# Fused decoder layer: K and Q projected transposed, split into bf16 pieces and stacked by DMA through DRAM, context laid out transposed, scatter indices copied early

## The chip, the cores and the metric

The kernel runs on one core of one Trainium2 chip, as a single launch. The metric is the device time of that launch in microseconds (us). Engines are named as in the profile: PE (TensorE), PEld (its weight load), DVE (VectorE), ACT (ScalarE), POOL (GpSimd), SP (SyncE, which here issues nearly all plain DMAs).

## What is computed

Four sequences (B = 4) of T = 512 tokens with D = 256 features pass through three layers. Cut to what matters:

```python
x_norm = layernorm(x); beta = x_norm @ w_in.T              # 1: recurrence, gate, MLP
c = chunked complex recurrence over beta (chunks of 64)
x1 = x + sigmoid(x_norm @ w_gate.T + b_gate) * (c @ w_out.T)
x  = layernorm(x1 + silu(layernorm(x1) @ w_mlp1.T + b1) @ w_mlp2.T + b2)

Q = x @ wq.T + bq; K = ctx @ wk.T + bk; V = ctx @ wv.T + bv   # 2: attention, 16 heads of 16
scores = causal((Q @ K.T) / 4); attn = softmax(scores)
x = layernorm(x + (attn @ V) @ wo.T + bo)

logits = x @ Wr.T       # 3: 48 experts, each takes its top 64 of the 2048 tokens
out = x + scatter_add(weight * expert(x[chosen]))     # expert: 256 -> 4 x 256 -> gelu -> 256
return layernorm(out)
```

The scores must keep nearly float32 accuracy, so each K and Q value is split into three bf16 pieces (first piece, the rounded rest, the rest of that). A head has 16 features; six products of pieces, (0,0) (1,0) (2,0) (0,1) (1,1) (0,2), are taken in one matmul by stacking six copies of 16 rows into 96 contraction rows (`SK`). Three more rows (`SX` = 99) subtract the row maximum, itself in three pieces, in the second pass: ones on the K side, minus the maximum on the Q side.

## The kernel before

It is written with five instruction streams and semaphores placed by hand. Each stream runs in the order of the code.

**Stage 1** (recurrence and MLP) runs over the four sequences. Its last part, `shrink(B - 1)`, is the second MLP matmul of the last sequence; the buffers `KTs` and `QTs` (stacked K and Q, features on partitions) share memory with the MLP weights, so nothing may be written there before it ends.

**Stage 2** (attention) handles the 16 heads of a sequence in four groups of four (`NG`, `GH`), and a group in four slots, one for each block of 128 tokens. In slot (g, j) PE makes the shifted scores of block j of group g (`shifted`, L1618), ACT takes exponentials (`exponentials`, L1301), POOL masks the diagonal (L683), PE multiplies with V (`values`, L1631). In the same slots PE makes the plain scores of the *next* group (`scores`, L1584 and L1588, two PSUM banks in turn), DVE takes their row maxima (`maxima`, L986), then negates and splits them (`negate`), and PE turns them (`minus_max`, L1600, copied by ACT, L1288). The next group's scores come in three shares a slot; slot 1 has shares of 2, 1 and 1 banks, slot 2 has one share of 4 banks. After each share come the steps that two tables name: `PREPARE` (for the next sequence) and `FINISH` (for this one). A bank is written again only when its maximum has been taken.

The loop over sequences runs three times (`Fori(0, B - 1)`), each turn with the groups in order 1, 2, 3, 0; group 0 of the first sequence stands ahead of the loop and groups 1 to 3 of the last sequence behind it, and those three have no `PREPARE` or `FINISH` steps.

What `PREPARE` does before: `context` and `query_in` turn the inputs on PE (L1512, ACT copies L1251); `key`, `query` (L1530) and `value` (L1550) project them with tokens on partitions; DVE adds the bias (L918, L938) and with ACT splits into pieces (`split_k`, `split_q`: L926, L930, L932, L933, L947 to L956 on DVE, L1259 to L1271 on ACT); `stack_k` and `stack_q`, 8 steps each per sequence, turn the stacked pieces on PE (`pe_stack`, L1564, 8 transposes a step), and ACT (K, L1276) or DVE (Q, L973) copies them to `KTs` and `QTs`. For the first sequence these steps are lists: `early` ahead of `shrink(B - 1)`, `late` (12 stack steps) behind it.

**Stage 3** (experts) handles 48 experts in 24 pairs. A ring of six weight buffers is refilled by SP (2.5 MB a pair) as PE frees them. For a pair p, POOL gathers 64 + 64 token rows by indirect DMA (`gather`, L720 copy of the indices, L723 DMA), PE turns them (L1740) and runs the expert, DVE weighs the result (L1153), and POOL adds the rows to `sums` in DRAM (`scatter`, L730 copy of the indices, L735 DMA). POOL's order is scatter p, gather p + 6, wait until scatter p has landed (`after_addition`), and on to p + 1: two scatters may hit the same row.

**Stage 4** reads `sums` back, adds, normalizes and stores.

## Time and profile before

| | us |
|---|---|
| three runs | 839.89, 836.05, 840.32 (median 839.89) |
| the profiled execution | 844.63 |
| its span, first to last instruction | 842.9 |
| mean granted PE clock | 0.895 of full speed |
| stage 1 | 0 to about 203 |
| stage 2 | about 203 to 571 |
| choice of tokens | about 571 to 611 |
| experts | about 611 to 818 |
| final sum and norm | about 818 to 843 |

Times inside the profile count from the start of the span. Busy shares of the span: PE 77%, DVE 47%, ACT 37%, POOL 22%. Many engines wait for each other in turn, so no single share says what a step is worth.

### The profile page before, as it was taken

How to read it: one execution, taken by the hardware profiler on the slowest of the kernel's cores; microseconds unless marked ns; L12 is line 12 of the kernel's file. 1: busy time of each engine (PE TensorE's matmuls, PEld its weight loads, DVE VectorE, ACT ScalarE, POOL GpSimd, SP SyncE). 2: the span in 40 equal slices, each digit the busy share in tenths (PEclk: the TensorE clock that was granted, in tenths of full speed). 3: DMA queues.
4: the chain of work that ended last, by engine and by line, in shares of the span. 5: the costliest groups of instructions: out<-in, count | busy, mean ns of one | idle time of the engine just before them, and what ended most of it. 6: DMA issues, size and time to landing. Idle time of an engine off the chain costs nothing.

```text
span 842.9 us, 13300 instructions
## 1 busy us (share of the span) xinstructions
PE 645.3 (77%) x4550; PEld 397.2 (47%) x4550; DVE 399.3 (47%) x837; ACT 307.9 (37%) x490; POOL 188.7 (22%) x250
## 2 busy tenths in 40 slices
PE   4599999999688887877787887851079987898920
PEld 2458575767355554645554554340035444454410
DVE  4534442524757564675647655427823322233315
ACT  2141414142364563546355545610023322232303
POOL 1322231400212111121102111200032224234424
PEclk9899999999699799989998999965579988999965
DMA  6830000110000002000020007018249998994238
GB/s 221 325 133 2 0 0 0 51 51 1 0 2 1 1 2 88 12 0 0 18 81 0 0 0 274 2 35 313 110 153 374 407 313 284 359 343 125 40 62 260
DMA packets 33010, 93.64 MB, mean 111 GB/s; under 512 B 2720, under 2 KB 24912, under 8 KB 29904
## 3 DMA queue, kind: packets, MB, share of 16 engines
q1 hardware_dynamic: 27664, 86.43, 27.6%
q0 software_dynamic: 4608, 6.29, 4.0%
q10 hardware_dynamic: 704, 0.47, 0.3%
q8 instruction: 20, 0.33, 0.2%
q14 instruction: 14, 0.11, 0.0%
HBM read 79.55 MB, written 11.53 MB: 108 GB/s over the span
## 4 chain that ended last, share of the span: by engine, by line
PE 47%; DVE 17%; DMA 15%; issue 10%; ACT 6%; POOL 3%; DVEq 0%; ACTq 0%; POOLq 0%; SPq 0%
DMA sums<-row 7%; PE PS L1457 7%; PE PS L1448 7%; PE PS L1530 5%; DMA sums<-wo_s,row 4%; PE PS L1754 4%; DVE Mx L986 3%; PE PS L1631 3%; PE PS L1564 2%; PE PS L1588 2%; PE PS L1618 2%; DMA wkv_s<-x_rows,row 2%; PE PS L1419 2%; PE PS L1436 2%; ACT arena L1301 2%
## 5 line engine op out<-in xcount | busy, mean ns | idle before, releaser
L986 DVE TENSOR_REDUCE Mx<-PS 128x1 f32<-128x384 f32 (+3 forms) x176 | 107.4, 638 | 85.6 <-PE PS L1588 84.7
L1301 ACT ACTIVATE arena<-PS 128x512 f32<-128x512 f32 (+1 forms) x176 | 86.3, 565 | 73.9 <-PE PS L1618 73.9
L683 POOL TENSOR_SCALAR_AFFINE_SELECT arena<-arena 128x512 f32<-128x512 f32 x64 | 40.9, 640 | 241.6 <-ACT arena L1301 241.6
L1618 PE MATMUL PS<-arena 99*128 99x512 bf16 (+3 forms) x256 | 58.6, 317 | 23.8 <-ACT arena L1301 16.9
L1588 PE MATMUL PS<-arena 96*128 96x128 bf16 (+3 forms) x256 | 66.5, 318 | 0.0
L1143 DVE TENSOR_TENSOR X<-PS,Y 128x512 f32<-128x512 f32 x48 | 31.3, 687 | 71.8 <-PE PS L1767 71.5
L1584 PE MATMUL PS<-causal,identb 128*128 128x128 bf16 (+2 forms) x176 | 45.5, 259 | 20.4 <-DVE Mx L986 17.8
L1448 PE MATMUL PS<-arena 128*128 128x512 f32 x128 | 55.8, 593 | 1.6 <-issue 1.6
L1457 PE MATMUL PS<-arena 128*128 128x256 f32 x256 | 55.9, 379 | 0.0
L1365 ACT ACTIVATE X<-X 128x512 f32<-128x512 f32 x48 | 29.5, 631 | 71.4 <-DVE X L1143 71.0
L1457 PEld LDWEIGHTS PS<-arena 128*128 128x128 f32 x256 | 48.6, 190 | 6.6
L1631 PE MATMUL PS<-arena 128*32 128x128 f32 (+3 forms) x512 | 49.7, 458 | 1.4 <-POOL arena L683 1.2
L1136 DVE COPY X<-PS 128x512 f32<-128x512 f32 x24 | 16.6, 692 | 65.9 <-PE PS L1754 63.6
L1754 PE MATMUL PS<-ring_a,X 128*64 128x512 f32 x192 | 46.5, 628 | 0.5 <-ACT X L1354 0.5
L1618 PEld LDWEIGHTS PS<-arena 99*128 99x128 bf16 x256 | 21.8, 100 | 50.8 <-ACT arena L1301 29.4
L1754 PE MATMUL PS<-arena,X 128*64 128x512 f32 x192 | 44.7, 608 | 0.0
L1584 PEld LDWEIGHTS PS<-causal,identb 128*128 128x128 bf16 x176 | 17.6, 100 | 56.1 <-DVE Mx L986 42.3
L1276 ACT ACTIVATE arena<-PS 99x1024 bf16<-99x1024 bf16 x32 | 31.8, 1025 | 33.3 <-PE PS L1564 33.2
L617 POOL TENSOR_SCALAR ve<-mv 128x4 f32<-128x4 f32 x16 | 3.7, 230 | 179.8 <-DVE mv L790 179.8
L1448 PEld LDWEIGHTS PS<-arena 128*128 128x128 f32 x128 | 24.2, 190 | 30.2 <-issue 29.5
L1288 ACT ACTIVATE arena<-PS 3x1024 bf16<-3x1024 bf16 x32 | 31.1, 1010 | 19.7 <-PE PS L1600 19.6
L1203 ACT ACTIVATE arena<-PS,vec 128x512 f32<-128x512 f32 x16 | 11.4, 775 | 71.7 <-PE PS L1403 71.7
(195 smaller groups left out, 1151.5 us busy)
## 6 DMA issues: line engine op xcount, KB each, us to landing
ring_a<-experts SPq DMA_DIRECT2D x12, 2048.0 KB, 10.9
arena<-experts SPq DMA_DIRECT2D x12, 2048.0 KB, 11.3
ring_a<-experts SPq DMA_DIRECT2D x12, 512.0 KB, 5.3
arena<-experts SPq DMA_DIRECT2D x12, 512.0 KB, 8.2
X<-x SPq DMA_DIRECT2D x4, 512.0 KB, 3.7
arena<-w_mlp SPq DMA_DIRECT2D x2, 1024.0 KB, 11.6
sums<-zrow SPq DMA_DIRECT2D x1, 2048.0 KB, 20.3
Y<-ctx_in SPq DMA_DIRECT2D x4, 512.0 KB, 4.7
```

Of the source, the lines that this page charges most:

```text
L683: pool.affine_select(out=pb[j % 2][:, :, 0:P], in_=pb[j % 2][:, :, 0:P], compare_op=ALU.is_ge, fill=0.0, base=0, pattern=[[0, GH], [1, P]] ...
L986: dve.tensor_reduce(Mx[:, g % 2, i, heads[0]:heads[-1] + 1], bank((g * NSH + u) % 2)[:, 0:len(heads) * w] .rearrange("p (h n) -> p h n", h ...
L1276: act.activation(KTs[0:SX, GH * q:GH * q + GH, 2 * P * m:2 * P * (m + 1)], spare(n).bitcast(BF16)[0:SX, :] .rearrange("p (h n) -> p h n", ...
L1301: act.activation(pb[j % 2][:, heads[0]:heads[-1] + 1, 0:w], bank(2 + n % 3)[:, 0:len(heads) * w] .rearrange("p (h n) -> p h n", h=len(heads)),
L1448: mm = pe.matmul(bank(HIDDEN[m % 4]), wm1_s[:, k, m * P:(m + 1) * P], xT2[:, k, :], start=(k == 0), stop=(k == KT - 1))
L1457: mm = pe.matmul(PS[:, 6 * 512 + t * D:6 * 512 + (t + 1) * D], hid[:, m, t * P:(t + 1) * P], wm2_s[:, m, :], start=(m == 0), stop=(m == MT ...
L1530: mm = pe.matmul(o[:, t * D:(t + 1) * D], xt[:, k, (2 * m + t) * P:(2 * m + t + 1) * P], w[:, k, :], start=(k == 0), stop=(k == KT - 1))
L1584: pe.matmul(o[:, 0:len(heads) * w].rearrange("p (h n) -> p h n", h=len(heads)) [:, :, i * P:w], identb[:], wide(causal[:], len(heads)), st ...
L1588: mm = pe.matmul(o[:, a * w:(a + 1) * w], QTs[0:SK, g * GH + h, i * P:(i + 1) * P], KTs[0:SK, g * GH + h, 0:w], start=False, stop=True, sk ...
L1618: mm = pe.matmul(bank(2 + n % 3)[:, a * w:(a + 1) * w], KTs[0:SX, g * GH + h, j * P:(j + 1) * P], QTs[0:SX, g * GH + h, j * P:T], start=Tr ...
L1631: mm = pe.matmul(bank(6)[VW * h:VW * (h + 1), j * P:T], Vb[:, j, g * GH + h, :], pb[j % 2][:, h, 0:T - j * P], start=(j == 0), stop=(j == ...
L1754: mm = pe.matmul(bank(1 + n)[CAP * e:CAP * (e + 1), :], xgT[:, k, CAP * e:CAP * (e + 1)], w1_of[u][:, e, k, n * 512:(n + 1) * 512], start= ...
```

## The change

It does five things.

1. The context arrives transposed (its layout is made on the host side of the inputs), so `context` steps, their PE transposes and ACT copies are gone. SP loads it straight to `cT`.
2. K and Q are projected with features on partitions (`pe_features`, two matmuls of 512 columns instead of four of 256). ACT makes the first piece from PSUM with the bias (`first_piece`), DVE the rest (`rest`, one operation with bias and subtraction), ACT the middle piece, DVE the last piece.
3. The stacking steps are gone from PE, ACT and DVE. SP writes the three pieces of K and of Q to DRAM (`split_out`) and reads them back, a group at a time, into the six row blocks of `KTs` and of `QTs` (`group_in`, 12 DMAs of 64 KB, 16 partitions each). `scores` waits for these. POOL writes the rows of ones into `KTs` once.
4. `value 0` moves from slot (1, 3) to slot (2, 1), `query_in 1` one slot ahead; for the first sequence key is ahead of the second half of the last MLP expansion and all that is left is ahead of `shrink(B - 1)`.
5. In stage 3 the scatter indices of pair p + 1 are copied ahead of the wait for scatter p (`rows_of`).

```diff
 PREPARE = {
-    (1, 0): ([("context", 0)], [], [("context", 1), ("query_in", 0)]),
-    (1, 1): ([("query_in", 1), ("key", 0)], [("key", 1), ("split_k", 0)],
-            [("split_k", 1), ("query", 0)]),
-    (1, 2): ([("split_k", 2)], [("query", 1)], [("split_k", 3), ("split_q", 0)]),
-    (1, 3): ([], [("split_q", 1)], [("split_q", 2), ("value", 0)]),
-    (2, 0): ([("split_q", 3)], [], []),
-    (2, 1): ([("stack_k", 0), ("stack_k", 1)], [], [("stack_q", 0)]),
...
+    (1, 0): ([("query_in", 0)], [], [("query_in", 1)]),
+    (1, 1): ([("key", 0)], [("key", 1)], [("query", 0)]),
+    (1, 2): ([("split_k", 0)], [("query", 1)], []),
+    (1, 3): ([("split_q", 0)], [], []),
+    (2, 1): ([], [("value", 0)], []),
 }
 ENTER = {
     (0, 0): ([], [], [("value", 1)]),
-    (0, 2): ([("stack_k", 6)], [("stack_k", 7), ("stack_q", 6)], []),
-    (0, 3): ([], [("stack_q", 7)], []),
 }
...
+            def split_out(b):
+                for g in kq_in:
+                    sp.wait_ge(g.s, g.before(b, NRD))
+                sp.wait_ge(ksd.s, ksd.now(b, KT + 1))
+                sp.dma_start(pieces_v[0], kp).then_inc(k_out.s, 16)
+                sp.wait_ge(qsd.s, qsd.now(b, KT + 1))
+                sp.dma_start(pieces_v[1], qp).then_inc(q_out.s, 16)
+
+            def group_in(b, g):
+                if g == 0:
+                    sp.wait_ge(k_out.s, k_out.now(b, 1))
+                    sp.wait_ge(q_out.s, q_out.now(b, 1))
+                sp.wait_ge(stm.s, stm.before(b, (g + 1) * NSH))
+                heads = slice(GH * g, GH * g + GH)
+                rows_g = slice(GH * HD * (g % 2), GH * HD * (g % 2) + GH * HD)
+                for n, (dst, order) in enumerate(((KTs, K_PIECES), (QTs, Q_PIECES))):
+                    for r, c in enumerate(order):
+                        sp.dma_start(dst[HD * r:HD * r + HD, heads, :],
+                                     pieces[n, c, g // 2, rows_g, :]
+                                     .rearrange("(h d) t -> d h t", d=HD)).then_inc(kq_in[g].s, 16)
...
+            tokens_in(0)
+            context_in(0)
+            split_out(0)
+            tokens_in(1)
+            sp.wait_ge(m2.s, m2.now(B - 1, 1))
+            for g in range(NG):
+                group_in(0, g)
+            context_in(1)
+
+            def relay(b, more=True):
+                split_out(b + 1)
+                group_in(b + 1, 0)
+                if more:
+                    tokens_in(b + 2)
+                for g in range(1, NG):
+                    group_in(b + 1, g)
+                if more:
+                    context_in(b + 2)
+                    outputs(b)
...
+            pool.wait_ge(m2.s, m2.now(B - 1, 1))
+            for g in range(NG):
+                pool.memset(KTs[SK:SX, GH * g:GH * g + GH, :], 1.0).then_inc(ones, 1)
+            pool.wait_ge(ones, NG)
             with_bias(0)
...
+            rows_of(0, 0)
             with pool.Fori(0, NP // RING - 1) as r:
                 for u in range(RING):
                     p = r * RING + u
                     scatter(p, u)
                     gather(p + RING, u, again=True)
+                    rows_of(p + 1, u + 1)
                     after_addition(p)
...
+            def rest(read, done, parts, left, bias):
+                def step(b, m):
+                    dve.wait_ge(read.s, read.now(b, m + 1))
+                    dve.wait_ge(done.s, done.before(b, KT + 1))
+                    dve.scalar_tensor_tensor(left[:, m, :], spare(m), vec[:, bias + m:bias + m + 1],
+                                             parts[:, 0, m, :], ALU.add, ALU.subtract)\
+                        .then_inc(done.s, 1)
+            def last_piece(read, done, parts, left):
+                def step(b, k):
+                    dve.wait_ge(read.s, read.now(b, KT + 1))
+                    dve.tensor_tensor(parts[:, 2], left, parts[:, 1], ALU.subtract)\
+                        .then_inc(done.s, 1)
...
+            def middle_piece(done, read, parts, left):
+                def step(b, k):
+                    act.wait_ge(done.s, done.now(b, KT))
+                    act.activation(parts[:, 1], left, ACT.Copy).then_inc(read.s, 1)
...
+            def pe_features(o, w, xt):
+                for k in range(KT):
+                    mm = pe.matmul(o, w[:, k, :], xt[:, k, :], start=(k == 0), stop=(k == KT - 1))
...
-                        pe.wait_ge(ske.s, ske.now(b, 2 * (g + 1)))
-                        pe.wait_ge(sqe.s, sqe.now(b, 2 * (g + 1)))
+                        pe.wait_ge(kq_in[g].s, kq_in[g].now(b, NRD))
...
             minus_max(0, 0)
+            pe.wait_ge(ones, NG)
             slots(0, pe_slot, first=True)
```

How the instruction order moves, at three places. First DVE in the loop, slots (1, 1) and (1, 2), where `arena` and `ring_a` hold the K and Q values. Before, from K's first subtraction on to Q's second bias addition:

```order
L926 TENSOR_TENSOR arena<-arena 128x1024 [waits ksa]
L937 ISA [waits qpr]
L938 TENSOR_TENSOR ring_a<-PS,row 128x512 [waits qsd]
L985 REGISTER_ALU
L986 TENSOR_REDUCE Mx<-PS 128x1 [waits smm]
...
L938 TENSOR_TENSOR ring_a<-PS,row 128x512 [waits qsd,qpr]
```

The same place in the changed kernel:

```order
L955 SCALAR_TENSOR_TENSOR ring_a<-PS,vec,ring_a 128x512 [waits qsd,qsa]
L964 REGISTER_ALU
L966 TENSOR_TENSOR arena<-arena 128x1024 [waits ksd,ksa]
L990 REGISTER_ALU
L991 TENSOR_REDUCE Mx<-PS 128x1 [waits smm]
...
L955 SCALAR_TENSOR_TENSOR ring_a<-PS,vec,ring_a 128x512 [waits qsd,qsa]
```

K's last piece (L966), which waits for ACT's middle piece (`ksa`), now stands ahead of the four maxima of slot (1, 2). Before, nothing stood between Q's first bias addition and these four.

Second POOL behind stage 1, before:

```order
L617 TENSOR_SCALAR ve<-mv 128x4 [waits vset,ln3]
L619 TENSOR_TENSOR rstd<-ve,mhalf 128x4 [waits rs3]
L676 TENSOR_TENSOR X<-X,row 128x1024 [waits rs3,xs_in]
L683 AFFINE_SELECT arena<-arena 128x4x128 [waits exq] x4
L695 UNCONDITIONAL_BRANCH
```

and in the changed kernel:

```order
L648 TENSOR_SCALAR ve<-mv 128x4 [waits ln3]
L650 TENSOR_TENSOR rstd<-ve,mhalf 128x4 [waits rs3]
L723 MEMSET arena 3x2048 [waits rs3,m2]
L723 MEMSET arena 3x2048 x3
L704 TENSOR_TENSOR X<-X,row 128x1024 [waits ones,xs_in]
```

The four memsets of the rows of ones stand behind the last normalization's square root, and PE waits for them (`ones`) ahead of its first slot.

Third POOL in the experts' loop, before (`row` is the memory of the index copies and of the results):

```order
L720 COPY row<-Y 128x1
L721 REGISTER_ALU
L723 DMA wkv_s<-x_rows,row 128x256 [waits gix]
L741 REGISTER_ALU
L730 ISA [waits scattered]
L730 COPY row<-Y 128x1
L733 REGISTER_ALU [waits six]
L735 DMA sums<-row 4096x256 [waits yws]
```

and in the changed kernel:

```order
L755 DMA wkv_s<-x_rows,row 128x256 [waits gix]
L761 ISA
L761 COPY row<-Y 128x1
L775 REGISTER_ALU
L767 REGISTER_ALU [waits scattered,six]
L769 DMA sums<-row 4096x256 [waits yws]
```

The copy (L730, now L761) has moved from behind the wait for `scattered` to ahead of it.

## Rows read from the trace of the kernel before

**Rows 1.** The page, mean busy share of the DMA engines, 40 slices of 21.1 us, tenths.

```profile
DMA  6830000110000002000020007018249998994238
```

**Rows 2.** Busy time by stretch: span, then PE, PEld, DVE, ACT, POOL, clock, DMA share.

```profile
359.50:379.90 20.40, 15.52 (x137) 8.92 (x136) 13.98 (x29) 10.93 (x18) 3.03 (x5) 0.83 0.00 0
379.90:397.40 17.50, 13.79 (x152) 8.74 (x153) 10.32 (x21) 11.46 (x19) 2.55 (x4) 1.00 0.00 0
397.40:424.80 27.40, 21.63 (x179) 14.21 (x179) 14.63 (x37) 12.13 (x20) 3.85 (x6) 1.00 0.17 46
424.80:448.60 23.80, 21.42 (x161) 14.87 (x161) 15.92 (x25) 13.34 (x22) 5.05 (x5) 1.00 0.09 35
527.20:540.10 12.90, 10.61 (x96) 5.30 (x96) 7.86 (x17) 7.86 (x15) 2.55 (x4) 1.00 0.01 2
```

**Rows 3.** Groups of instructions by line, 356.3 to 445.6 us, one loop turn.

```profile
L1564 PE MATMUL PS<-identb,arena 128*99 128x128 bf16 x64 | 5.5, 243 | 0.6 <-DVE Y L1015 0.6
L1550 PE MATMUL PS<-wkv_s,arena 128*128 128x128 f32 x32 | 4.0, 278 | 0.0
L1512 PE MATMUL PS<-ident,Y 128*128 128x128 f32 x24 | 3.6, 277 | 0.8 <-DVE Y L1015 0.8
```

**Rows 4.** Timeline of the loop: start, us, engine, line, [idle before and releaser].

```profile
419.84 0.44 PE L1600 MATMUL PS<-identb,nst 128*3 128x128 bf16 x5 [1.59 <-DVE arena L973]
...
439.47 2.52 DVE L986 TENSOR_REDUCE Mx<-PS 128x1 f32<-128x512 f32 x4
439.95 1.06 ACT L1262 ACTIVATE arena<-arena 128x1024 bf16<-128x1024 f32 x1
444.37 1.23 DVE L930 TENSOR_TENSOR arena<-arena 128x1024 bf16<-128x1024 f32 x1
...
452.52 0.39 PE L1618 MATMUL PS<-arena 99*128 99x512 bf16 x1 [2.87 <-ACT arena L1301]
```

**Rows 5.** Timeline between stage 1 and the loop, PE and POOL.

```profile
166.50 1.81 POOL L659 MEMSET arena<- 128x2048 f32 x1
189.58 13.98 PE L1457 MATMUL PS<-arena 128*128 128x256 f32 x64
...
213.95 0.38 PE L1584 MATMUL PS<-causal,identb 128*128 128x512 bf16 x1 [0.83 <-DVE arena L973]
224.98 1.04 POOL L619 TENSOR_TENSOR rstd<-ve,mhalf 128x4 f32<-128x4 f32 x1
225.70 1.03 PE L1618 MATMUL PS<-arena 99*128 99x512 bf16 x2 [1.16 <-ACT arena L1288]
```

**Rows 6.** DMA to landing (the page), and SP's time for an issue (min/median/max ns).

```profile
x_rows<-ring_a SPq DMA_DIRECT2D x4, 512.0 KB, 3.0
L529 SPq DMA_DIRECT2D x_rows<-ring_a x4: 380/390/407, 330.1 to 565.9; - x4
```

**Rows 7.** Experts: timeline of scatters (POOL) and results (DVE), and PE's waits.

```profile
632.89 1.65 POOL L735 DMA_INDIRECT sums<-wo_s,row  x1 [9.63 <-DVE wo_s L1153]
...
645.13 1.61 POOL L735 DMA_INDIRECT sums<-wo_s,row  x1 [1.01 <-POOL row L730]
651.59 0.47 DVE L1153 TENSOR_SCALAR row<-PS,Y 128x256 f32<-128x256 f32 x1
658.27 0.47 DVE L1153 TENSOR_SCALAR row<-PS,Y 128x256 f32<-128x256 f32 x1
...
757.43 1.60 POOL L735 DMA_INDIRECT sums<-wo_s,row  x1 [1.01 <-PE PS L1740]
...
807.54 0.48 DVE L1153 TENSOR_SCALAR row<-PS,Y 128x256 f32<-128x256 f32 x1 [2.41 <-PE PS L1786]
PE PS L1740 <- DMA wkv_s<-x_rows,row: 22.4, 6, 5.8
```

**Rows 8.** The chain that ended last, in the tail of the scatters: start, us, what.

```profile
793.00 3.84 DMA sums<-wo_s,row
...
814.12 3.80 DMA sums<-row
```

More of the change, by code:

```diff
@@ L31 @@
 SX = SK + NPC
+K_PIECES = (0, 1, 2, 0, 1, 0)
+Q_PIECES = (0, 0, 0, 1, 1, 2)
+NRD = 2 * NPR
 VW = 32
@@ L468, in all_steps @@
             return [step for lists in table.values() for names in lists for step in names]
-        after = ("stack_k", 0), ("stack_q", 0)
-        first_steps = all_steps(PREPARE)
-        split_at = min(first_steps.index(step) for step in after)
-        early = [(name, 0, k) for name, k in first_steps[:split_at]]
-        late = [(name, 0, k) for name, k in first_steps[split_at:]]
+        early = [(name, 0, k) for name in ("query_in", "key") for k in range(KT)]
+        late = [("split_k", 0, 0), ("query", 0, 0), ("query", 0, 1), ("split_q", 0, 0),
+                ("value", 0, 0)]
         block = stack.enter_context(nc.Block())
@@ L533, in _ @@
             sp.wait_ge(res.s, res.now(B - 1, 3))
-            inputs(0)
-            with sp.Fori(0, B - 1) as b:
-                inputs(b + 1)
-                outputs(b)
-            sp.wait_ge(skt.s, skt.now(B - 1, 2 * NG))
+            tokens_in(0)
[16 more added lines that the diff above has]
+                    outputs(b)
+            with sp.Fori(0, B - 2) as b:
+                relay(b)
+            relay(B - 2, more=False)
+            weights(0, 0, second=False)
             sp.wait_ge(vpr.s, vpr.now(B - 1, 2))
+            outputs(B - 2)
             weights(3, 3)
-            sp.wait_ge(sqt.s, sqt.now(B - 1, 2 * NG))
-            weights(0, 0, second=False)
             outputs(B - 1)
@@ L958, in dve_value @@
+            def last_piece(read, done, parts, left):
+                def step(b, k):
+                    dve.wait_ge(read.s, read.now(b, KT + 1))
+                    dve.wait_ge(done.s, done.now(b, KT))
+                    dve.tensor_tensor(parts[:, 2], left, parts[:, 1], ALU.subtract)\
+                        .then_inc(done.s, 1)
+                return step
             def dve_value(b, m):
```

238 lines of the change are left out of this document (77 added, 161 removed).

## The prediction

> **What bounds the kernel now.** I read the slices of the page first, then busy time by stretch, then the timeline of the places that the change touches, then the waits. The DMA slices [rows 1] show where transfers can matter: nearly none in the attention (the tenth to the twenty-seventh slice), and 8 or 9 tenths through most of the experts' stage. In the attention no engine is full: a turn of the loop is a ring of PE, DVE, ACT and POOL, and its length is what the ring adds up to. The stretches of one turn [rows 2] are the measure: group 2 takes 20.4 us, group 3 17.5, group 0 27.4, group 1 23.8. The last sequence, whose groups have the same scores, maxima and exponentials but no step of either table, gives the bare group: 12.9 us. What a turn can win by losing steps is read against this number and not against busy shares.
>
> In the experts' stage PE waits for no weights. It waits for gathered rows: 22.4 us in 6 waits, of which 5.8 is the first fill [rows 7]. A gather is issued right behind a scatter, and a scatter only when the one before has landed and its index copy is done. So the scatters are a chain: the first starts at 632.89, the fourteenth at 757.43, 9.6 us apart, while PE undisturbed gives a result each 6.7 us (651.59, 658.27). In each link stand the copy, some 0.2 us, and the 1.01 us from its end to the DMA behind it, 1.2 in all [rows 7].
>
> **The attention loop, group by group.** *Group 2* loses five stack steps and gains `value 0`. Bare group plus one value step, half of the 4.0 us of L1550 [rows 3]: 14.9. The bare group runs at full clock; today's group 2 has a granted clock of 0.83 [rows 2], because DVE's split copies hold up the maxima and PE stands for 2.87 us [rows 4]. Both go. 20.4 to 14.9. *Group 3* loses seven stack steps and has nothing left: 17.5 to 12.9. *Group 0* keeps value, heads, output, norm, turn and logits and loses four stack steps: K's eight steps cost PE 5.5 us busy (L1564 [rows 3]), so four steps at most 2.8, less where they overlap; the 1.59 us wait for a stack copy [rows 4] also goes, but DVE's statistics hold the maxima there, so not all of both is won. I take 2.4: 25.0.
>
> *Group 1* is where the change can lose. It sheds the context's eight transposes (of 24 of L1512 in 3.6 us [rows 3], 1.2 busy, I take 0.9) and `value 0` (2.0, moved). But in slot (1, 2) K's last piece now stands ahead of four maxima on DVE and waits for ACT's middle piece, which waits behind two exponentials. I follow it with today's times, shifted by the 0.9: PE ends the slot's shifted scores at 438.1; ACT first owes Q's first piece, then exponentials to 439.4, then the middle piece (1.06, as L1262 today) to 440.5; DVE's last piece (1.23, as L930) to 441.8; so the first of the four maxima starts at 441.8 where today the four start at 439.47 [rows 4]. PE has two banks, so it stands from 438.7 to the end of the first maximum, 442.5: a hole of 3.8 us with nothing behind it in its queue that could run, for the second query projection stands behind the four scores. After that, query 1, its first piece on ACT, its rest on DVE, the negation, the turn of the maxima and ACT's copies follow in series, with ACT's middle piece of Q (1.06) ahead of the copies. My hand count puts the next group's start at 450.2 against 448.4 to 448.6 today, so group 1 is 25.4 at full clock. Today's hole of 2.87 us is followed by a lower clock; a hole of 3.8 probably is too, and I add 2.0 for matmuls at the low level (bounds 0 and 3.3, the time PE loses behind today's hole). Group 1: 27.4, from 23.8.
>
> Sum of a turn: 27.4 + 14.9 + 12.9 + 25.0 = 80.2 against 89.1, 8.9 saved; three turns: **27 us**. Without hole and low clock it would be 13 a turn (39). If only the 4.6 of group 3 and the 2.4 of group 0 came and the rest were eaten up by group 1, 5 a turn (15).
>
> **What the DMAs cost.** No row shows a 64 KB DMA onto 16 partitions. From below: SP issues in 0.39 us and 512 KB in 1 KB rows land in 3.0 [rows 6], so a group's twelve are 4.7 us of issue plus some 2.5 to land, 7 us. From above: each of the twelve takes its landing alone, 3.0, so 36 us. The last row blocks overlap in the queue as the weights do today, so I take the nearer end, 8 us. In the loop, Q's last piece is ready at about 449.5, the pieces' write lands some 5 us later, group 0's rows at 462.5, and PE wants them one bare group and a value step after 450.2, at 465. Margin 2.5 us: hidden, but only just. The other three groups are read a group or more ahead. SP's other DMAs wait behind these, but the context and token loads are wanted a group later.
>
> SBUF — State Buffer, a page of the Trainium skill, section "Door 1: The DMA port swizzle (why `[64,N]` ≈ `[32,N]`)", says that a transfer to partitions 0 to 15 reaches 4 of 16 ports, about 109 GB/s, and a later section of it that transfers to different partitions do not add up. By that rule a 64 KB transfer would hold the queue for 0.6 us (an estimate from the page's figure), twelve would take 7.2 plus the landing, and the rows would come about 1.5 us later than in my sum, still inside the margin; nothing in this trace shows it.
>
> **Between stage 1 and the loop.** Today `shrink` ends at 203.56, twelve stack steps follow, and the scores start at 213.95 [rows 5]. Then: the context's transposes and a wait are gone ahead of `shrink`, so it ends 1.7 us earlier, at 201.9; then one group's DMAs, 8 to 9.2 us: scores at 210.5, 3.4 earlier. PE stands longer and starts at the lower clock, which gives 0.7 back. But the first slot now waits for the ones. POOL writes them only after the root of the last norm, which ends at 226.0 today and 2.7 earlier then, at 223.3. The nearest memset is 128 x 2048 f32 in 1.81 us [rows 5]; 3 x 2048 bf16 has as many elements on a partition, so I take 1.75 each, four times: 7.0 (bounds: half of it, if bf16 goes twice as fast, and 7.2). PE starts at 230.5 where today it starts at 225.70, 4.8 later. Four stack steps less in that group and a norm that no longer holds DVE give 2.8 back. **Net +2** (from -3.6 to +5).
>
> **Experts.** The removed 1.2 us (I use 1.13, as a short check of the semaphore stays) stands in each link. Thirteen links up to the scatter at 757.43 make 14.7 us if the DMAs land as fast as today. They will not quite: a faster chain means that PE asks sooner for weights, and the DMA engines are 8 to 9 tenths busy [rows 1]. Bounds 0 and 14.7; I take 0.7 a link, **9 us**. In the tail the last result is ready at 808.02 while the last scatter starts at 814.12 [rows 7]: the last five scatters start 5.3 us apart (793.00 to 814.12 [rows 8]), so the chain lags behind PE's results. With links of 3.84 + 0.3 [rows 8] it catches up, the last two results 2.9 apart: the last scatter starts some 2 us behind its result and lands 3.9 earlier relative to PE. Experts together: **13 us** (4 to 19).
>
> **Sum.** -27 + 2 - 13 = -38. The profiled execution took 844.63 (span 842.9 and 1.7 around it), so 806.6. The median of the three runs is 839.89, 4.7 lower; the forecast for the median is **802**.
>
> **Rivals.**
> *The relay comes late (slower).* If a 64 KB DMA holds the queue for d us, group 0's rows come in 12 d + 2.5. Beyond d = 0.6 each turn loses 12 (d - 0.6) minus what is left of the margin (1.5), and the start loses the same once without margin. With d = 1.5 that is 3 x 9.3 + 10.8 = 39, and the saving of 38 is gone; with d = 1.7 it is 48, so 850. The page's port rule stands for d = 0.6 alone. For it speaks that a row block's descriptors all end on few partitions, against it that 512 KB in equally small rows land in 3.0 [rows 6], which is d = 0.4 even with the fixed part in it. 8%, 850.
> *Attention gives less.* The bare group is measured where SP is quiet and no table has steps; if group 1 stretches by a further 4 us, or the relay is a little late in each turn, the loop brings 12 and the total is 817. 14%.
> *The experts' chain gains nothing.* Every 1.13 us saved is given back by longer landings, since the DMA engines are the real limit; only the tail's 4 stay: 811. For it speak the 9 tenths [rows 1], against it that the first link took 12.2 us and the mean one 9.6 [rows 7]: later landings were much shorter, so the engines are not full throughout. 12%.
> *My forecast,* 66%, 785 to 812.
>
> **Range.** The least is all of the loop (39), 19 in the experts and 3.6 at the start: 62, 778. The most inside the eight in ten takes the rival of a weaker attention with half the experts' gain: 824. So 779 to 824. Faster or slower by 0.5% (4.2 us) is what a measurement can tell from no change. Faster: 0.66 + 0.14 + 0.12 less a little for their bad ends, 0.88; slower 0.08; same 0.04.
>
> **What the profile will show.** Group stretches of about 27, 15, 13 and 25 us, twelve DMAs of 64 KB at some 0.4 us issue each, no PE wait on them in the loop, a hole of 3 to 4 us on PE in slot (1, 2) with four maxima released by the last piece (L966), four memsets of about 1.75 us with PE waiting for POOL ahead of its first slot, scatter links 0.5 to 1 us shorter, and a last scatter within 3 us of the last result. I am wrong if PE waits for SP's DMAs at the first scores of a group, if group 2 and 3 stay above 16 and 14, or if the landings of the scatters grow by as much as the copy gave.

## The result and the profile after

The changed kernel takes 815.63 us (median of 4 runs, 810.62 to 816.48), the kernel before 840.07 (4 runs, 836.05 to 840.32): ratio 0.970 with a 95% interval of 0.966 to 0.974, so 24 us faster. The forecast was 802 with a range of 779 to 824. The profiled execution took 816.48, its span is 814.7 and its mean granted clock 0.884; it stands against the 844.63 of before, 28.2 less, where the sum had 38. All medians here are of executions in the chip's usual state; three slower ones (819.0 us of `e3_ones_early`, 931.7 and 843.7 us of the kernel before) are left out.

The page of the changed kernel, granted PE clock and busy share of the DMA engines by slices of 20.4 us, beside [rows 1]. The relay fills the tenth to the twenty-third slice with up to 4 tenths. The busiest slices of the experts' stage show 59999994 where they showed 49998994. (The 7 tenths of the twenty-fifth slice in [rows 1], which the prediction counts as nearly none, are the experts' first weights.)

```profile
PEclk9899999999569899989998989965589999898965
DMA  6840000003410341134113334018159999994247
```

Busy time by stretch in the changed kernel, the second turn of the loop in the order of groups 1, 2, 3, 0, then the bare group of the last sequence; columns as in [rows 2].

```profile
329.33:356.94 27.61, 21.02 (x120) 9.84 (x120) 13.19 (x23) 13.96 (x24) 2.55 (x4) 0.88 0.09 28
356.94:371.65 14.71, 12.36 (x111) 7.16 (x111) 8.74 (x21) 7.80 (x15) 4.89 (x5) 1.00 0.56 178
371.65:384.67 13.02, 10.58 (x96) 5.30 (x96) 7.86 (x17) 7.81 (x15) 2.55 (x4) 1.00 0.36 106
384.67:411.16 26.49, 21.03 (x147) 13.27 (x148) 13.50 (x35) 9.99 (x18) 3.80 (x6) 0.94 0.23 77
506.82:519.68 12.86, 10.60 (x95) 5.28 (x95) 7.86 (x17) 7.82 (x15) 2.55 (x4) 1.00 0.01 2
```

Read against [rows 2], groups 2 and 3 fell to the forecast's 14.9 and 12.9 within 0.2 us. Group 1 grew by 3.8 to 27.6 and its clock fell to 0.88. Group 0 won only 0.9, and its clock, 1.00 before, is 0.94: PE is busy for 21.03 us against 21.63, although four stack steps are gone (one took some 0.5). A turn is 81.8 us, before 89.1.

The timeline of the changed kernel, first between stage 1 and the loop, then slot (1, 2) of the second turn, then slot (0, 2) of the first. Each row is start, duration, engine, line, and in brackets the idle time before it with its releaser.

```profile
202.16 22.79 SPq L537 DMA_DIRECT2D arena<-pieces  x48
209.76 0.59 PE L1563 MATMUL PS<-causal,identb 128*128 128x512 bf16 x1 [7.63 <-DMA arena<-pieces]
223.02 6.09 DVE L837 TENSOR_SCALAR X<-X,mv,rstd 128x256 f32<-128x256 f32 x4 [1.58 <-POOL rstd L650]
223.30 7.55 POOL L723 MEMSET arena<- 3x2048 bf16 x4 [0.32 <-POOL rstd L650]
230.90 1.04 PE L1597 MATMUL PS<-arena 99*128 99x512 bf16 x2 [9.41 <-POOL arena L723]
...
344.98 1.23 DVE L966 TENSOR_TENSOR arena<-arena 128x1024 bf16<-128x1024 f32 x1 [1.17 <-ACT arena L1268]
346.12 1.28 DVE L991 TENSOR_REDUCE Mx<-PS 128x1 f32<-128x512 f32 x2
346.86 0.29 PE L1563 MATMUL PS<-causal,identb 128*128 128x128 bf16 x1 [3.57 <-DVE Mx L991]
347.97 3.62 PE L1526 MATMUL PS<-arena,wq_s 128*128 128x512 f32 x4
...
317.13 1.41 DVE L824 BATCH_NORM_STATS2 stats<-ring_a 128x6 f32<-128x256 f32 x4
318.99 2.49 DVE L991 TENSOR_REDUCE Mx<-PS 128x1 f32<-128x512 f32 x4
319.70 0.23 PE L1563 MATMUL PS<-causal,identb 128*128 128x128 bf16 x1 [2.59 <-DVE Mx L991]
```

These are the places that the forecast named. The scores begin at 209.76 (forecast 210.5), the first slot at 230.90 behind the memsets (forecast 230.5). In slot (1, 2) K's last piece (L966) runs ahead of the maxima and PE stands 3.57 us (forecast 3.8); behind it the four matmuls of the second query projection (L1526) take 3.62 us, elsewhere 1.88: the low level, 1.2 GHz. The last block is what the forecast saw only in part: DVE's statistics and aggregation stand ahead of the maxima of slot (0, 2) too, as they did before, and the hole that PE has there has grown to 2.59 us.

The experts in the changed kernel, scatters (POOL) and the last result (DVE), beside [rows 7, 8].

```profile
611.00 1.65 POOL L769 DMA_INDIRECT sums<-wo_s,row  x1 [9.30 <-DVE wo_s L1157]
...
729.71 1.60 POOL L769 DMA_INDIRECT sums<-wo_s,row  x1 [4.03 <-issue]
...
782.30 0.48 DVE L1157 TENSOR_SCALAR row<-PS,Y 128x256 f32<-128x256 f32 x1 [3.47 <-PE PS L1762]
784.39 1.57 POOL L769 DMA_INDIRECT sums<-row  x1 [2.99 <-DMA sums<-row]
```

From the first to the fourteenth scatter it is 118.7 us, before 124.5: 9.13 a link against 9.58, so 0.45 won where the forecast took 0.7. The last scatter starts 2.1 us behind the start of its result's row, before 6.6.

### The profile page after: what moved, and what is told of

The parts are those of the page before. It is cut to its first block, busy times and chain, and to the rows that moved or that the text cites. A ratio compares the mean times of both kernels' runs of the same rounds, so it can differ in the third digit from the quotient of the medians.

```text
span 814.7 us, 12126 instructions
## 1 busy us (share of the span) xinstructions
PE 612.5 (75%) x3942; PEld 351.0 (43%) x3942; DVE 358.4 (44%) x777; ACT 274.5 (34%) x458; POOL 195.1 (24%) x253
## 4 chain that ended last, share of the span: by engine, by line
PE 49%; DMA 16%; DVE 15%; issue 9%; ACT 7%; POOL 3%; SPq 1%; ACTq 0%; DVEq 0%; POOLq 0%
DMA sums<-row 9%; PE PS L1451 7%; PE PS L1442 7%; DMA sums<-wo_s,row 4%; DVE Mx L991 4%; PE PS L1730 4%; PE PS L1526 4%; PE PS L1610 3%; PE PS L1597 3%; PE PS L1567 3%; PE PS L1518 2%; PE PS L1413 2%; PE PS L1430 2%; PE PS L1563 2%; PE PS L1545 2%
## 5 line engine op out<-in xcount | busy, mean ns | idle before, releaser
L1597 PE MATMUL PS<-arena 99*128 99x512 bf16 (+3 forms) x256 | 55.8, 307 | 26.3 <-ACT arena L1279 12.6
L1610 PE MATMUL PS<-arena 128*32 128x128 f32 (+3 forms) x512 | 52.3, 481 | 1.0 <-POOL arena L711 0.9
L769 POOL DMA_INDIRECT sums<-row x16 | 25.6, 1597 | 64.6 <-issue 43.8
```

What stands on the lines that cost most here:

```text
L1597: mm = pe.matmul(bank(2 + n % 3)[:, a * w:(a + 1) * w], KTs[0:SX, g * GH + h, j * P:(j + 1) * P], QTs[0:SX, g * GH + h, j * P:T], start=Tr ...
L1610: mm = pe.matmul(bank(6)[VW * h:VW * (h + 1), j * P:T], Vb[:, j, g * GH + h, :], pb[j % 2][:, h, 0:T - j * P], start=(j == 0), stop=(j == ...
```

## The experiments

Each median stands against the kernel before on the same chip (836.1 to 841.3) or the changed kernel's 815.6. The changed kernel was not run again beside the experiments, and the kernel before differs by 5 us between the chips, so a difference of 4 us or less to the 815.6 says little by itself; the spans inside the profiles say more.

**The two halves apart.** `e1_indices_alone` is the kernel before with only the early copy; `e2_attention_alone` is the changed kernel without it.

```diff
+            rows_of(0, 0)
...
                     gather(p + RING, u, again=True)
+                    rows_of(p + 1, u + 1)
                     after_addition(p)
```

> The kernel before with only the early copy of the scatter indices. Theory: the copy stands in each link of the scatters, but the landings give half of it back, so 13 links win about 0.45 us each (5.8) and the last scatter follows its result by under 2 us instead of 6.1 (some 3 to 4 more at the end): 8 to 9 us, a median of 831 to 832. First gather unchanged against before. Rival: the DMA engines are the limit and only the tail wins, 836. Second rival: the whole 1.13 us comes in each link when the attention is as before, 14.7 plus 4, 821.

> The changed kernel with the copy of the scatter indices put back behind the wait. Theory: the two halves of the change add up. The first gather stays at about 590, 21.6 us earlier than before, and from there on everything is as before: 840 - 21.6 = 818.5, or 824 if the 8.1 us of the experts are lost on 815.6. Both ends are within 818 to 824. Rival: the early attention changes the experts' stage by itself (other phase of weights and scatters), then the sum of this gain and of the indices' own gain differs from the whole 24.4 by more than 4 us.

First, fourteenth and last scatter of the attention alone, then of the indices alone:

```profile
609.36 1.65 POOL L770 DMA_INDIRECT sums<-wo_s,row  x1 [9.27 <-DVE wo_s L1154]
736.34 1.60 POOL L770 DMA_INDIRECT sums<-wo_s,row  x1 [1.01 <-DVE row L1154]
792.37 1.57 POOL L770 DMA_INDIRECT sums<-row  x1 [0.89 <-POOL row L761]
```

```profile
632.05 1.65 POOL L738 DMA_INDIRECT sums<-wo_s,row  x1 [9.52 <-DVE wo_s L1160]
747.51 1.60 POOL L738 DMA_INDIRECT sums<-wo_s,row  x1 [5.65 <-DVE row L1160]
801.16 1.57 POOL L738 DMA_INDIRECT sums<-row  x1 [3.01 <-DMA sums<-row]
```

The attention alone: 821.9 us, ratio 0.979 (0.974 to 0.984), so 17 us, as expected. The indices alone: 835.1, ratio 0.994 (0.991 to 0.998), so 4 to 5 us where 8 to 9 were expected; by its median this is nearer to the rival in which only the tail wins. In its profiled execution first to last scatter fell from 181.2 to 169.1 us, more than the medians show. One execution is a poor measure of this stage: over the ten kernels with an early copy and full weights that this study profiled, the stretch is 168.0 to 178.3 (mean 174.1); with a late copy, two, it is 181.2 and 183.0. The mean gain is 8 us by these (5 up to the fourteenth scatter and 3 behind it), 4 to 6 by the medians (835.1 against 838.8, 815.6 against 821.9), and 13 was forecast. The halves add up to 21 of the 24 us, within what they can be told apart.

**What a link is made of.** `e7a_after_quarter` and `e7b_before_quarter` load a quarter of each refilled weight block of the experts; they leave out the other three quarters, so their results are not the layer's.

```diff
-                    weights(u, r * RING + u, second=False)
+                    sp.dma_start(slot[u][:, 0:W1C // 4], experts[r * RING + u][:, 0:W1C // 4])\
+                        .then_inc(w1_ring[u].s, 16)
...
+                    (the same for the second part)
```

> The changed kernel, whose refills of the expert ring load only a quarter of each weight block, so that the experts from the seventh pair on compute with weights that are not theirs; it leaves out three quarters of the bytes and nothing else. Theory: the landings of the scatters are long because the weights load at the same time; without them a scatter lands in about 3.9 us, a link is shorter than the 6.5 us that PE needs for a pair, and PE sets the pace: first to last scatter some 150 us instead of 173.4, a median of 790 to 795. Rival: the landing is the scatter's own (4096 small additions into DRAM) and stays at 8 us on average: first to last scatter 165 or more, a median above 805.

> The kernel before, with the same three quarters of the refilled weight bytes left out. With e7a it tells what the place of the index copy is worth when the DMA engines are nearly idle. Theory: the link (1.6 + 1.2 for the copy + 3.9 us of landing) is still about PE's pace, so the place of the copy changes only the tail: first to last scatter within 3 us of the changed kernel's with a quarter of the bytes, and the medians differ by the attention's 17 to 21 us plus at most 3. Rival: the copy's 1.13 us stand in each link whatever the load: first to last scatter some 20 us or more apart.

Two neighbouring scatters of each, the changed kernel first:

```profile
615.00 1.61 POOL L772 DMA_INDIRECT sums<-wo_s,row  x1 [2.73 <-DVE wo_s L1160]
621.68 1.60 POOL L772 DMA_INDIRECT sums<-row  x1 [2.83 <-DVE row L1160]
```

```profile
639.35 1.61 POOL L738 DMA_INDIRECT sums<-wo_s,row  x1 [2.29 <-DVE wo_s L1156]
643.39 0.18 POOL L733 COPY row<-Y 128x1 uint32 x1 [0.39 <-DMA sums<-wo_s,row]
646.04 1.60 POOL L738 DMA_INDIRECT sums<-row  x1 [2.46 <-DVE row L1156]
```

791.0 and 814.9 us. With this lighter weight traffic (140 GB/s in the stretch of 632 to 695 us, at a DMA share of 0.59, so not idle) every scatter lands in 3.7 to 4.0 us and a link is 6.68 us in both, PE's pace: the scatter is released by DVE's result and no longer by the landing before it, the late copy (643.39) is done 2.5 us before it is wanted, and first to last scatter is 151.1 and 151.3 us. Both theories held; the medians are 23.9 apart. The stage's excess over 151, 23 us with the early copy and 31 with the late one, comes with the full traffic, under which a scatter takes 4.7 to 12.4 us to land up to the fourteenth. In the same stretch of 632 to 695 us the DMA engines of the changed kernel are busy all the time:

```profile
632.00:695.00 63.00, 57.04 (x482) 29.66 (x480) 19.75 (x33) 17.65 (x32) 21.14 (x28) 0.95 1.00 375
```

What the place of the copy is worth in a link can be read from the chain that ended last, the first link of the kernel before and of the changed kernel (start, us, what; a DMA's time is that to its landing):

```profile
632.89 10.80 DMA sums<-wo_s,row
644.34 0.58 issue
```

```profile
611.00 8.91 DMA sums<-wo_s,row
620.20 0.58 issue
621.00 11.18 DMA sums<-wo_s,row
```

Before, the landing is at 643.69 and the next scatter at 645.13 [rows 7], 1.44 us later; in the changed kernel it is 619.91 and 621.00, 1.09. Over the thirteen links the means are 1.47 and 1.14. The two profiles with a late copy have 1.47 and the ten with an early one 1.13 or 1.14. So the early copy takes 0.33 us out of a link and not 1.13: the 0.58 us of `issue`, in which POOL waits for nothing that the profile shows, stand between landing and scatter in either order. The landings themselves did not grow: 8.11 us in the mean of the thirteen before, 8.00 in the changed kernel; over the two late profiles 8.2, over the ten early ones 8.2 (7.7 to 8.6).

**The ones.** `e3_ones_early` puts the four memsets ahead of the root of the last norm.

```diff
+            pool.wait_ge(vset, 2)
+            pool.wait_ge(m2.s, m2.now(B - 1, 1))
+            for g in range(NG):
+                pool.memset(KTs[SK:SX, GH * g:GH * g + GH, :], 1.0).then_inc(ones, 1)
+            pool.wait_ge(ones, NG)
             root(ln3, rs3, B - 1, 1 + 2 * TT)
```

> The changed kernel with the four memsets of the rows of ones put ahead of the square root of the last norm on POOL, where POOL has nothing to do (202 to 221 us). PE then no longer waits 9.41 us ahead of its first slot. Theory: the first slot starts at about 222.7 instead of 230.9, but the last norm (6.09 us from 223.02) now stands ahead of group 1's first maximum on DVE, which comes at 229.1 instead of 232.9, and PE gets some of its slot's own work done before: 4 to 6 us are won, a median of 811. Rival: what was waiting for the ones waits for DVE and for the loop's first turn in the same way, under 2 us, 814 or more. Second rival: all 8.2 come, 807.5.

```profile
202.53 7.04 POOL L696 MEMSET arena<- 3x2048 bf16 x4 [34.15 <-PE PS L1453]
222.94 1.01 PE L1599 MATMUL PS<-arena 99*128 99x512 bf16 x2 [1.21 <-issue]
223.24 3.41 DVE L839 TENSOR_SCALAR X<-X,mv,rstd 128x256 f32<-128x256 f32 x4 [1.57 <-POOL rstd L650]
```

806.4 us, 9.2 less, as the second rival had it, and my 4 to 6 was too low. I had left the norm on DVE at its 6.09 us; without the memsets beside it, it takes 3.41. By the profiles the first slot starts 8.0 us earlier and group 1 6.4 earlier (241.94 instead of 248.31), so 6.4 us are located; the loop behind it is 2.3 shorter too, but that is no work of this edit, for `e2` and `e7a`, with the changed kernel's attention, have such a loop as well.

**The hole in slot (1, 2).** `e4_split_behind`:

```diff
-    (1, 2): ([("split_k", 0)], [("query", 1)], []),
+    (1, 2): ([], [("query", 1)], [("split_k", 0)]),
```

> The changed kernel with K's last piece (and ACT's middle piece) moved from ahead of the four maxima of slot (1, 2) to behind the negation. Theory: the hole of 3.57 us on PE and the low granted clock behind it are what makes group 1 26.8 us; without them it is about 22 (4 to 5 us a turn, three turns): a median of 801 to 804, group 1 at a clock near 1.00. K's pieces are written some 5 us later, still before Q's, so group 0's rows come in time. Rival: the hole only moves, because the turn of the maxima and the second query's rest follow in series: 0 to 2 us a turn, 810 to 816. Second rival: the relay becomes late and PE waits for SP's DMAs at the first score of group 0: 816 or more.

Group 1 of the second turn by stretch, and PE behind its first maximum in slot (1, 2):

```profile
325.52:348.52 23.00, 18.45 (x120) 9.01 (x120) 13.45 (x23) 13.85 (x24) 3.54 (x4) 1.00 0.03 10
```

```profile
340.65 0.23 PE L1563 MATMUL PS<-causal,identb 128*128 128x128 bf16 x1 [1.17 <-DVE Mx L991]
341.53 1.88 PE L1526 MATMUL PS<-arena,wq_s 128*128 128x512 f32 x4
```

799.3 us, 16 less, a little below what was expected. Group 1 falls from 27.3 to 22.7 us in the mean of three turns (4.6 a turn, 13.8 in all; against `e2` and `e7a`, whose group 1 is 26.8, it is 4.1 a turn and 12 in all). In the second turn 2.4 is the hole (3.57 to 1.17) and 2.2 stands behind it, 1.7 of which is the four matmuls of L1526, 1.88 us again where they took 3.62 at the low level; the clock is now 1.00. No wait for the relay appeared in the loop.

**The hole in slot (0, 2).** `e5_stats_behind`:

```diff
-    (0, 1): ([("heads", 1)], [("output", 0)], [("output", 1), ("stats", 0)]),
-    (0, 2): ([], [], [("norm", 0)]),
+    (0, 1): ([("heads", 1)], [("output", 0)], [("output", 1)]),
+    (0, 2): ([], [], [("stats", 0), ("norm", 0)]),
```

> The changed kernel with the last norm's statistics of a sequence moved from ahead of the four maxima of slot (0, 2) to behind the negation of that slot. In the changed kernel PE stands 2.59 us there, and for the next 4 us the granted clock is 0.77. Theory: group 0 is bound by the series output, statistics, root, norm, turn, logits as much as by its maxima; the hole goes, but the norm comes 1.5 to 2 us later and PE waits for it ahead of the last turn: group 0 stays within 1 us of 26.5, and the median within 3 us of the changed kernel's 815.6. Rival: as in slot (1, 2), what stands ahead of the maxima is the whole price of the group: group 0 falls by 2.5 us or more, a median of 808 or less.

```profile
318.15 0.23 PE L1563 MATMUL PS<-causal,identb 128*128 128x128 bf16 x1 [0.53 <-DVE Mx L991]
...
324.38 0.64 POOL L711 TENSOR_SCALAR_AFFINE_SELECT arena<-arena 128x512 f32<-128x512 f32 x1
325.07 0.42 PE L1610 MATMUL PS<-arena 128*32 128x128 f32 x8 [2.58 <-POOL arena L711]
328.09 3.29 PE L1639 MATMUL PS<-arena,wr_s 128*64 128x512 f32 x4 [0.74 <-ACT arena L1251]
```

822.3 us, 6.7 more: both expectations missed (beside its own chip's kernel before the ratio is 0.982, the changed kernel's was 0.970). The hole at the maxima is gone (0.53), but POOL's root, in its queue ahead of the mask of slot (0, 3), now comes late; PE waits 2.58 us for that mask, and the logits behind it run at the low level (3.29 against 1.93). Group 0 is 28.0 to 29.2 us. A hole cannot be cured by moving DVE's step alone; what POOL has queued behind its part comes with it.

**The relay.** `e6_relay_halves` issues 24 reads of 32 KB a group instead of 12 of 64 KB.

```diff
+                        for half in range(2):
+                            h0 = GH * g + 2 * half
...
-                        sp.dma_start(dst[HD * r:HD * r + HD, heads, :],
+                            sp.dma_start(dst[HD * r:HD * r + HD, h0:h0 + 2, :],
```

> The changed kernel with each 64 KB read of the relay issued as two of 32 KB (24 a group instead of 12, the same bytes). It asks what a relay DMA costs, an issue or its bytes, and how much slack the loop has. In the changed kernel the twelve of group 0 are issued from 278.2 to 284.8, the last lands 2.3 us later at about 287, and PE wants them at about 290. Theory: SP's issue of 0.47 to 0.55 us each is the price, whatever the size; group 0's rows land at about 292.5 to 293.5, PE waits 2 to 4 us for them in each of three turns, and the first scores start 6 to 7 us later: 815.6 + 14 to 19, a median of 830 to 835. Rival: the bytes are the price, then the issues shrink with the size, and nothing is longer: 816 to 818.

```profile
284.04 11.81 SPq L538 DMA_DIRECT2D arena<-pieces  x24
...
297.41 0.60 PE L1565 MATMUL PS<-causal,identb 128*128 128x512 bf16 x1 [1.20 <-DMA arena<-pieces]
```

823.7 us. The issues still follow each other by 0.46 to 0.49 us for half the bytes, and the first slot comes 6.0 us later, as the theory said. In the loop I was wrong: PE waits 1.20, 0.37 and 0.27 us for the rows, where 2 to 4 was expected in each turn. Group 3, in which the wait falls, is 2.7 us longer in the first turn, where its clock is 0.89, and 0.5 and 0.4 in the other two at 1.00. The margin had been larger than I thought: in the changed kernel the last read of group 0 is issued at 284.3 and lands some 2.3 later, at 286.6, and PE wants it at 290.3: 3.7 us, forecast 2.5.

**The moves together.** `e7_both` joins `e3` and `e4`. `e8_stats_split` adds that the first two of four statistics are taken right behind the first half of the output:

```diff
                                   X[:, bass.ds(b * TT + 2 * m, 2), :], ALU.add).then_inc(ln4.s, 1)
+                dve.wait_ge(ln4.s, ln4.now(b, 3 * m + 1))
+                for t in (2 * m, 2 * m + 1):
+                    dve.bn_stats(stats[:, t, :], x2b[:, t, :]).then_inc(ln4.s, 1)
```

> The changed kernel with both moves: the memsets of the ones ahead of the last norm's root, and K's last piece behind the negation of slot (1, 2). Theory: the two stand in different places and add up; alone they gave 8.6 and 16.3 us, so 815.6 - 24.9 = 790.7, first gather some 22 us ahead of the changed kernel's. Rival: part of the first gain came from group 1 of the first turn, which the second also shortens, or the experts' stage gives some of it back: 795 or more.

> The kernel with both moves, and the last norm's statistics of the first two token tiles taken right behind the first half of the output, where DVE has nothing to do, so that two of four statistics stand ahead of the maxima of slot (0, 2) instead of four. Theory: two statistics (0.7 us) less in the series that group 0 waits for, the hole on PE in slot (0, 2) falls from 2.6 to 1.9 us, and some of the low clock behind it goes too: 0.7 to 1.5 us a turn, three turns, 2 to 4 us below the kernel with both moves. Rival: the hole stays long enough for the clock to fall as before, or the chain of the norm sets the end in any case: under 1 us.

Group 0 of the second turn in `e8_stats_split`, and PE behind its first maximum of slot (0, 2):

```profile
368.52:393.82 25.30, 21.27 (x147) 13.15 (x147) 13.13 (x35) 10.10 (x18) 3.84 (x6) 0.93 0.25 80
```

```profile
308.33 0.23 PE L1570 MATMUL PS<-causal,identb 128*128 128x128 bf16 x1 [1.82 <-DVE Mx L993]
```

793.7 and 791.4 us. The first is 3 above its sum; its first gather comes 17.9 us ahead of the changed kernel's, where 22 was expected, and the scatters take the usual 174.4. Group 0 fell from 26.4 to 25.4 in the mean of the turns, as expected; the hole is 1.82, the clock still 0.93. The medians (4 runs each, 791.5 to 798.3 and 785.4 to 795.8) do not tell the two apart; the spans of group 0 do. `e8_stats_split` has the lowest median of all, ratio 0.943 (0.936 to 0.951) to the kernel before, 24 us below the changed kernel.

**Two queues.** `e9_two_queues` adds that ACT's queue issues the six query blocks of the first group; in `e10_queues_alone` SP waits for these twelve before it reads the next group.

```diff
+            for r, c in enumerate(Q_PIECES):
+                act.dma_start(QTs[HD * r:HD * r + HD, 0:GH, :],
+                              pieces[1, c, 0, 0:GH * HD, :].rearrange("(h d) t -> d h t", d=HD))\
+                    .then_inc(kq_in[0].s, 16)
```

> The kernel of the run before it, with the six query row blocks of the first group of the first sequence issued by ACT's queue beside SP's six. Between 202 and 220 us ACT has nothing to do. Theory: an issue of 0.47 us is the price of a relay DMA, and two queues issue side by side: the first scores start 2.8 us earlier (six issues), and the end comes 2 to 3 us earlier. Rival: the DMAs or the descriptors share one limit, whatever queue issues them: under 1 us.

> The two-queue kernel, with SP holding back the second group's reads until the first group's twelve have landed, so that the first twelve (six from each queue) have the DMA engines to themselves. In the two-queue kernel the scores began no earlier (8.8 us of wait for the rows against 7.6 with one queue), and in that stretch the DMA engines were 9 tenths busy or more at some 150 GB/s, where one queue gave some 140 GB/s at 4 to 6 tenths. Theory: what those transfers share is a ceiling of some 160 GB/s for rows that end on 16 partitions, so 786 KB take 4.9 us plus some 2 to land, 6.9 us; the wait ahead of the first scores is within 0.8 us of 7.6. Rival: it was only the second group's reads that took the engines; then six issues of 0.47 and one landing make 5.1 us, and the wait is 5.5 or less. In neither case does the median move by more than 3 us from the two-queue kernel's 795.

The stretch in which the rows land, by one queue (`e8_stats_split`), then by two (`e10_queues_alone`); the last two columns are the DMA engines' busy share and GB/s.

```profile
204.00:209.60 5.60, 0.00 (x0) 0.00 (x0) 0.05 (x1) 0.00 (x0) 5.60 (x4) 0.86 0.47 138
```

```profile
204.00:209.60 5.60, 0.00 (x0) 0.00 (x0) 0.09 (x1) 0.00 (x0) 5.60 (x4) 0.86 1.07 130
```

795.0 and 795.4 us, and PE waits 8.81 and 8.40 us for the rows where one queue took 7.61: nothing won. Two queues move no more bytes in a second (130 GB/s against 138); the engines only count as busy twice as long. The theory of `e9` fell. That of `e10` held, just (8.40 is within 0.8 of 7.6), with a ceiling of 130 GB/s and not 160. At 64 KB the two limits nearly meet: 0.47 us from issue to issue, and 0.50 us a transfer at 130 GB/s; at 32 KB the issue alone sets the pace.

## Why the prediction was right, and where its sizes were off

By the profiled executions, which the sum was made for: between stage 1 and the loop +2.05 us (group 1 starts at 248.31, before at 246.26; forecast +2). The loop, to group 1 of the last sequence, -22.4 (forecast -27; `e2` and `e7a`, with the same attention, need 242.3 and 242.1 us for it against 245.0 here, so in them it is -25). Behind it to the first gather -1.2 (nothing forecast). First gather to landing of the last scatter -8.1 (forecast -13). Sums and final norm +1.5 (nothing forecast: the eight reads of `sums` took 15.5 us instead of 14.4; in `e2` and `e3` they take 14.4 and this part is as long as before, so it belongs to this one execution). Together -28.2 against -38.

**Group 2, group 3, the start.** Right to 0.2 us a group. What made it so was the bare group as a measure: 12.9 us before, 12.86 after. The price of the memset, 1.75 us from an f32 one with as many elements, was 1.76 where POOL ran alone (7.04 for four, `e3_ones_early`).

**Group 1.** The hole of 3.8 us was 3.57, the 2.0 added for the low level stands against 1.7 in the four matmuls behind it, the group 27.3 in the mean (forecast 27.4; 26.8 in `e2` and `e7a`), and `e4_split_behind` takes just this away. The forecast had the change's main fault in the loop by place and by size; the fault cost 12 to 14 of the 39 us that the loop could have brought.

**Group 0** is the step that failed: "I take 2.4: 25.0". It is 26.6 in the mean of three turns, so 0.8 was won, 4.8 us less over the loop (26.2 in `e2` and `e7a`, so 1.2 and 3.6 less). The working took PE's busy time and one wait off the group, and saw that the statistics hold the maxima there, but not how much of the stack steps stood in waits for DVE. The same place in the second turn, first in the trace of the kernel before, then in the changed kernel's:

```profile
410.89 0.61 PE L1564 MATMUL PS<-identb,arena 128*99 128x128 bf16 x8
...
414.19 0.23 PE L1584 MATMUL PS<-causal,identb 128*128 128x128 bf16 x1 [2.13 <-DVE Mx L986]
...
417.64 0.61 PE L1600 MATMUL PS<-identb,nst 128*3 128x128 bf16 x8
```

```profile
404.39 1.54 PE L1579 MATMUL PS<-identb,nst 128*3 128x128 bf16 x13 [0.70 <-DVE nst L1009]
```

The hole was there before too, 2.13 us, and the stack step ahead of it (L1564) took 0.45 until the next row; it has not become time saved but idle time, 2.58: the hole ends 16.80 us into the group before and 16.87 after. The turn of the maxima (L1600, now L1579) starts 20.25 us into the group before and 19.72 after, now behind a wait for DVE's split: three more stack steps were worth 0.5 us together. From there to the group's end it is 7.19 and 6.77 us. The 1.59 us wait went, but 3.4 us of work at the low level (404.1 to 407.5) took most of it back. That the longer hole brought the low level is not shown: `e1_indices_alone`, with the attention of before and its hole of 2.13, has the same 3.4 us at the low level in two of three turns, where the group takes 27.6 us instead of 27.4. The rest of the group hangs on the chain of output, statistics, root, norm, turn and logits: `e5_stats_behind` (longer when the statistics come later) and `e8_stats_split` (1.0 us a turn shorter when half come earlier) are in line with this, but neither parts it from the hole and from POOL's mask.

**The relay.** Hidden in the loop, as forecast, with 3.7 us of margin instead of 2.5. By the Trainium skill, page SBUF — State Buffer, section "Door 1: The DMA port swizzle (why `[64,N]` ≈ `[32,N]`)", a transfer to partitions 0 to 15 reaches 4 of 16 ports, about 109 GB/s; the traces show 130 (two queues) and 138 (one) with rows for six such blocks one behind the other, so they agree in kind, and the estimate of 0.6 us from the page's figure is 0.1 too long. Its section "Can I just issue two DMAs to hit both halves?", and DMA: Bandwidth & Descriptors, section "Issuing engines are not separate DMA queues", say that a second queue brings next to nothing; `e9_two_queues` and `e10_queues_alone` agree, at 130 against 138 GB/s.

**Experts.** The second step that was off: "The removed 1.2 us (I use 1.13 ...) stands in each link", and with it "I take 0.7 a link". The reading of [rows 7] took all of POOL's 1.01 us between the copy and the scatter for a cost of the copy. It is not: the time from a landing to the next scatter fell from 1.47 to 1.14 us, so 0.33 a link was there to win, 4.3 us in thirteen links, where the forecast had 14.7 as its bound and took 9. The 0.45 a link between the two profiles is this and 0.11 of shorter landings. The forecast's reason for taking less than 1.13, longer landings, did not come either (8.11 and 8.00 us). So the rival "the experts' chain gains nothing" was wrong in its mechanism, though its 4 us for the experts was no farther from the 8 of the profiles than my 13. `e7a` and `e7b` show that the chain binds only under the full weight traffic: without it the place of the copy is worth 0.2 us. What in that traffic lengthens a landing, the DMA engines or the DRAM behind them, was not tried. In the tail the lag behind the last result fell by 4.5 us (forecast 4), but from the fourteenth to the last scatter only 2.0 were won (56.7 to 54.7 us), 3 in the mean of the profiles.

**The median.** The sum gave 806.6 for a profiled execution, and I took 4.7 off because before's stood that much above its median. The changed kernel's stood 0.9 above. These 3.8 us are the rest of the 13.6 between 802 and 815.6. So the loop's mechanism was right and carried the result; that the experts' term, read more than three times too large for a link, did not push the total out of the range is in part luck and in part the range's width of 45 us.

## What to carry to other kernels

Of each step that goes, ask what it costs and also what it covers: here removed PE steps lay inside waits for DVE, and without them PE only stood longer. Put what nobody waits for soon (K's last piece) behind what PE waits for at once (the maxima), on each in-order queue, and place one-time writes (the ones) where their engine is idle anyway; these two moves, one line and five, gave 22 us together, nearly as much as the whole change. And what moving an instruction out of each link of a chain is worth is read from the landing to the next start, before and after (1.47 and 1.14 us here); the idle time shown behind the instruction (1.01) can belong to the one that follows, and then it stays.

## What the hardware showed that was not expected

- POOL's memsets and DVE's norm slow each other: four `tensor_scalar` of 128 x 256 f32 take 6.09 us beside four memsets, 3.41 beside one addition on POOL, and 1.75 in slot (0, 2) with a short root ahead and little beside them (322.34 us of the changed kernel); the memsets take 7.55 beside the norm and 7.04 without. The Trainium skill, SBUF — State Buffer, section "Who interferes with whom", says that VectorE and GpSimd share a pair of SBUF ports, and that when a VectorE instruction works in a mode with two ports (`tensor_scalar` can) whoever issues first holds the pair for its whole instruction. The rows agree in kind; no run here tells the ports from another cause.
- The busy share of the DMA engines says little about bytes: 0.47 and 1.07 at the same 130 to 138 GB/s, for the same transfers from one queue and from two.
- A 64 KB DMA in 1 KB rows to 16 partitions lands in 2.3 us, one of 32 KB in 1.8, both in the median. SP's issue takes 0.43 and 0.42 us, and the next follows after 0.47 (up to 0.55 in the mean of a group of twelve); for 512 KB with 128 partitions the issue had taken 0.39 [rows 6].
- An indirect scatter-add of 128 rows of 1 KB lands in 3.7 to 4.0 us beside 140 GB/s of weight loads, and in 4.7 to 12.4, 8 in the mean, beside some 350 to 390 GB/s.
